# A recurrent cell with a chosen weight set: gate columns in groups of 256, 128 and 128, and the input-gate term written into PSUM by ScalarE

## The chip, the cores and the metric

One core of a Trainium2 chip runs the whole program. The metric is the device time of one execution in microseconds (us). The kernel before takes 7033.68 us, the median of 2 runs (7032.79 and 7034.57).

## The reference, cut to what matters

The program is a chain of eight layers over 625 nodes of 512 features. The change lies in one of them, a recurrent layer that walks over the 625 rows one after the other. At each row it first chooses one of four cells from the state, and then applies that cell alone:

```python
def step(carry, x_t):
    h, c = carry
    logits = concatenate([h, c, x_t]) @ W_sel.T + b_sel      # 4 logits
    s = argmax(logits)                                       # the chosen cell
    g = x_t @ W_ih[s] + h @ W_hh[s] + b_ih[s] + b_hh[s]      # 2048 values: i, f, g, o
    i, f, g, o = split(g, 4)
    c2 = sigmoid(f) * c + sigmoid(i) * tanh(g)
    h2 = sigmoid(o) * tanh(c2)
    return (h2, c2), h2
```

Nothing of a step can begin before the h and c of the step before it are there, and the cell is known only when the logits are.

## The kernel before, in words

`stage_lstm` (L1517 to L1845) holds the recurrence. TensorE, VectorE, ScalarE, GpSimd and SyncE each run a program of their own, which semaphores keep together; the order on each engine is that of the code, written out by hand. The loops hold `UN = 2` steps each: 312 turns of two steps after a first cell. The products with the input, `x_t @ W_ih` for all cells, lie ready in device memory (`xg`); SyncE loads the 64 values per partition of a coming step into `xg_buf`.

On TensorE a step goes as follows (`turn_of_two`, L1759 on).

- The logits: one matmul for the input's share (L1764), four with the new c as weights (L1767, after `c_ready`), four with tanh(c) as weights (L1772, after `w_ready` and `tanh_c`). They are 32-bit, so each is two passes, and leaves two weight loads and two matmuls in the trace.
- The products with h: h stands as two 16-bit parts in `h_pair`, four columns of weights, and W_hh streams past. A group of them (`products`, L1774) is four matmuls side by side on the four column quarters of the array, one for each quarter j of 512 gate columns. The 512 columns are cut in two: the first `FIRST = 320` go into `ps_rows`, the other 192 into `ps_rows_last`. A full sum is eight groups (two parts of W_hh, four chunks of h).
- The first `AHEAD = 2` chunks are multiplied for all four cells before the choice is known: 8 groups of 320 columns. Then TensorE waits for `best` (the index that VectorE finds, L1642), loads the index into a register and branches into one of four copies of `recurrent` (L1802): 6 more groups of 320 columns, 8 groups of 192 columns, and four 32-bit matmuls with a unit matrix that put the chosen cell's input term into `ps_gates` (L1806).
- The turns: the rows of gates (4 partitions wide) are copied to `gate_rows` by ScalarE (320 columns, L1701) and VectorE (192 columns, L1649), and 16 small 32-bit matmuls with `l_gsel` turn them into columns and add them to `ps_gates` (L1823): 10 after ScalarE's copy (`evac_a`), 6 after VectorE's (`evac_v`).
- The late products: two 32-bit matmuls of 156 columns (L1835) per step, a piece of `x @ W_ih` for rows that come much later.

The gate values are interleaved: each of the 16 columns of `ps_gates` holds one gate of one chunk, and a quarter of 512 columns mixes the gates. So ScalarE's tanh over all 16 columns (L1685) waits for all turns. Then come on VectorE the input and forget part (L1626), the output gate (L1627), the new c (L1629) and the gated selection weights (L1631); on ScalarE tanh(c) (L1687); on VectorE h twice and its second 16-bit part (L1634, L1635, L1637), which TensorE's next groups wait for (`hp_ready`). ScalarE follows the same branch as TensorE (L1695 to L1714), since which cell's rows it copies depends on the index.

Of the kernel before, what the change touches and what calls it, by code (L numbers as in the profile page):

```python
# [1426 lines left out]
GATE_SLOT = (0, 1, 3, 2)  # L1427
SLOT_GATE = (0, 1, 3, 2)
# [5 lines left out]
def stage_input_gates(nc, xt, wih_in, bias_a_in, bias_b_in, bias, scale, xg):  # L1434
# [4 lines left out]
    with ExitStack() as ctx:  # L1439
# [10 lines left out]
        with nc.Block() as block:  # L1450
# [32 lines left out]
            def _(v):  # L1483
                nc.vector.memset(scale[:], 0.5).then_inc(S["bias"], 1)
                v.wait_ge(S["bias"], 1)
                nc.vector.memset(scale[:].rearrange("p (s q) -> p s q", s=CELLS)[:, :, 3 * KC:], 1.0).then_inc(S["bias"], 1)
# [37 lines left out]
def stage_lstm(nc, whh, xt, wih_in, bias, scale, xg, xsel, pairs, wsel, ident, gsel, hist):  # L1524
# [9 lines left out]
    FIRST = 5 * 64  # L1534
    assert 1 + LOOPS * UN == N
    TURNS, PER, GROUP = BLOCK // UN, KC // UN, 2 * KC
    with ExitStack() as ctx:
        def sb(name, shape, dt=F32):
            return ctx.enter_context(nc.sbuf_tensor(name, shape, dt))
        xgb = sb("xg_buf", [128, UN, 2, CELLS * 8])  # L1540
# [4 lines left out]
        act = sb("gates_and_c", [128, 20])  # L1545
        ccur = act[:, 16:20]
# [9 lines left out]
        psg = ctx.enter_context(nc.psum_tensor("ps_rows", [128, CELLS * BANK], F32))  # L1556
        psb = ctx.enter_context(nc.psum_tensor("ps_rows_last", [128, BANK], F32))
        psc, psl = (ctx.enter_context(nc.psum_tensor(n, [128, BANK], F32)) for n in ("ps_gates", "ps_logits"))
# [4 lines left out]
            "xg0_in", "init", "c_ready", "o", "w_ready", "h_made", "hp_ready", "logits", "best", "rows_first", "rows_last", "evac_a", "evac_v",  # L1563
            "gates", "acted", "fi", "tanh_c", "kept", "seen_v", "seen_a", "seen_g", "seen_pe", "xg_used", "late_used", "late_moved", "late_stored")}
        with nc.Block() as block:
            @block.sync
            def _(sp):
                sp.dma_start(xg0[:].rearrange("p (h e) -> p h e", h=2), xg[0, :, :, 0, :].rearrange("h p e -> p h e")).then_inc(S["xg0_in"], 16)

                def load_gates(g, token):  # L1570

                    for h in range(2):
                        sp.dma_start(xgb[:, g, h, :].rearrange("p (s e) -> p s e", s=CELLS), xg[:, h, :, ds(token, 1), :].rearrange("s p t e -> p s (t e)")).then_inc(xg_in[g], 16)
# [40 lines left out]
            def _(v):  # L1614
                nc.vector.memset(hpair[:], 0.0).then_inc(S["init"], 1)
                for e in range(CELLS):
                    nc.vector.memset(psg[:, e * BANK:(e + 1) * BANK], 0.0).then_inc(S["init"], 1)
                nc.vector.memset(psb[:], 0.0).then_inc(S["init"], 1)
                nc.vector.memset(ccur, 0.0).then_inc(S["init"], 1)
                v.wait_ge(S["init"], CELLS + 3)  # L1620

                def cell(k):
# [8 lines left out]
                    nc.vector.tensor_tensor(wgated[:], wsel[:, 0:KC, :], ok[:].unsqueeze(2).broadcast_to([128, KC, PAIRS]), ALU.mult).then_inc(S["w_ready"], 1)  # L1631

# [49 lines left out]
            def _(a):  # L1682
                def cell(k):
                    a.wait_ge(S["gates"], k + 1)
                    nc.scalar.activation(act[:, 0:16], psc[:, 0:16], ACT.Tanh).then_inc(S["acted"], 1)  # L1685
# [4 lines left out]
                with a.Fori(0, LOOPS) as i:  # L1690
                    for q in range(UN):
# [58 lines left out]
            def _(pe):  # L1750
                pe.wait_ge(S["init"], CELLS + 3)
# [6 lines left out]
                nc.tensor.matmul(psc[:, 0:16], ident[:], xg0[:], start=True, stop=True).then_inc(S["gates"], 1)  # L1758
                def turn_of_two(i, token):  # L1759

                    for q in range(UN):
# [13 lines left out]
                        def products(e, part, c, out, lo, hi):  # L1775

                            for j in range(4):
                                at = e * CELL_COLS + (part * KC + c) * GATES + j * D
                                m = nc.tensor.matmul(out[32 * j:32 * j + 4, :], hpair[:, c, 2 - 2 * part:6 - 2 * part], whh[:, at + lo:at + hi],  # L1779
                                                     start=(part == 0 and c == 0), stop=(part == 1 and c == KC - 1), skip_group_check=True)  # L1780
                            return m

                        def first(e, part, c):

                            return products(e, part, c, psg[:, e * BANK:e * BANK + FIRST], 0, FIRST)

# [8 lines left out]
                        def recurrent(e):  # L1795
# [24 lines left out]
                        def turn(c, quarters=range(4)):  # L1820

                            for j in quarters:
                                m = nc.tensor.matmul(psc[32 * j:32 * j + 32, c:16:4], gsb[:, c * 128 + 32 * j:c * 128 + 32 * j + 32], gsel[:], start=False, stop=(c == KC - 1), skip_group_check=True)  # L1823
                            return m

# [511 lines left out]
```

## Time and profile before

| what | value |
|---|---|
| median of 2 runs | 7033.68 us |
| profiled execution, own time | 7026.58 us |
| its span in the trace | 7024.9 us |
| TensorE busy (matmul) | 6144.5 us, 87% of the span |
| VectorE, ScalarE, GpSimd busy | 2459.5, 1721.2, 928.1 us |
| mean granted TensorE clock | 0.961 of full |
| recurrent stage in the trace | about 3584 to 6660 us |

Busy time of TensorE includes the draining of its pipeline, so it is no measure of how close the engine is to its limit. In a step of a few microseconds, what matters is the order of the waits: which engine stands idle until which event. The profile's line number is that of the instruction's source line, so all products with h stand under L1779, told apart by the PSUM tile that they write.

### The profile page before, as it was taken

How to read it: one execution, taken by the hardware profiler on the slowest of the kernel's cores; microseconds unless marked ns; L12 is line 12 of the kernel's file. 1: busy time of each engine (PE TensorE's matmuls, PEld its weight loads, DVE VectorE, ACT ScalarE, POOL GpSimd, SP SyncE). 2: the span in 40 equal slices, each digit the busy share in tenths (PEclk: the TensorE clock that was granted, in tenths of full speed). 3: DMA queues.
4: the chain of work that ended last, by engine and by line, in shares of the span. 5: the costliest groups of instructions: out<-in, count | busy, mean ns of one | idle time of the engine just before them, and what ended most of it. 6: DMA issues, size and time to landing. Idle time of an engine off the chain costs nothing. (4 is left out here: it accounts for less than half of the span.)

```text
span 7024.9 us, 492334 instructions
## 1 busy us (share of the span) xinstructions
PE 6144.5 (87%) x210539; PEld 4079.7 (58%) x210539; DVE 2459.5 (35%) x11546; ACT 1721.2 (25%) x8472; POOL 928.1 (13%) x2082
## 2 busy tenths in 40 slices
PE   6856999999999999998789999999999999999852
PEld 5523555555555545544467777777777777777631
DVE  5324545455542211111233332333333332222248
ACT  0121333333333333333011111111111111111112
POOL 0011111111118820000000000000000000000003
PEclk9977999999999999999799999999999999999975
DMA  1011111111111100000232221222112221111100
GB/s 48 1 45 35 33 33 34 33 34 33 34 35 42 42 7 0 0 0 0 71 94 41 40 41 16 40 41 45 22 31 44 42 35 7 7 7 7 16 20 8
DMA packets 806866, 204.14 MB, mean 29 GB/s; under 512 B 701431, under 2 KB 766683, under 8 KB 806804
## 3 DMA queue, kind: packets, MB, share of 16 engines
q1 hardware_dynamic: 764500, 151.79, 11.3%
q0 software_dynamic: 41152, 46.42, 2.4%
q10 hardware_dynamic: 1152, 5.15, 0.2%
q8 instruction: 35, 0.57, 0.0%
q14 instruction: 27, 0.22, 0.0%
HBM read 174.86 MB, written 28.16 MB: 29 GB/s over the span
## 5 line engine op out<-in xcount | busy, mean ns | idle before, releaser
L1779 PE MATMUL ps_rows<-whh,h_pair 128*4 128x320 f16 x34944 | 1305.9, 299 | 84.2 <-issue 2.4
L1095 PE MATMUL ode_busy<-ode_busy_x,ode_busy_w 128*32 128x320 f16 (+4 forms) x19248 | 1244.8, 320 | 9.1 <-PEq L1031 7.1
L1779 PEld LDWEIGHTS ps_rows<-whh,h_pair 128*4 128x4 f16 x34944 | 735.2, 84 | 511.0 <-DVE h_pair L1637 154.2
L1089 PEld LDWEIGHTS ode_psa<-ode_a,ode_w2t 128*32 128x32 f32 x19968 | 396.6, 108 | 770.8 <-ACT ode_a L1204 573.2
L1649 DVE COPY gate_rows<-ps_rows_last 128x192 f32<-128x192 f32 x624 | 222.9, 357 | 1511.8 <-PE ps_rows_last L1779 1511.8
L1214 DVE SCALAR_TENSOR_TENSOR ode_part<-ode_b 128x1 f32<-128x1 f32 x624 | 111.5, 179 | 1645.1 <-ACT ode_b L1206 1643.3
L1701 ACT COPY gate_rows<-ps_rows 128x320 f32<-128x320 f32 x624 | 265.8, 426 | 1676.7 <-PE ps_rows L1779 1676.7
L1089 PE MATMUL ode_psa<-ode_a,ode_w2t 128*32 128x1 f32 x19968 | 607.0, 181 | 49.4 <-ACT ode_a L1198 43.2
L1206 ACT ACTIVATE ode_b<-ode_psa 128x1 f32<-128x1 f32 x2496 | 427.4, 171 | 815.9 <-PE ode_psa L1089 799.1
L1823 PE MATMUL ps_gates<-l_gsel,gate_rows 128*32 128x4 f32 x19968 | 397.4, 176 | 147.2 <-DVE gate_rows L1649 147.1
L1779 PE MATMUL ps_rows_last<-whh,h_pair 128*4 128x192 f16 x19968 | 521.4, 246 | 0.0
L1835 PE MATMUL ps_late<-l_xt,late_w 128*128 x2496 | 496.6, 321 | 0.0
L1106 PE MATMUL ode_pso<-whh 125*32 125x170 f32 (+1 forms) x8160 | 473.7, 310 | 0.0
L1204 ACT ACTIVATE ode_a<-ode_psu 128x1 f32<-128x1 f32 x1872 | 320.9, 171 | 595.9 <-PE ode_psu L1089 595.9
L1089 PE MATMUL ode_psa<-ode_ones,ode_b_parts 128*32 128x1 bf16 x9988 | 458.3, 163 | 0.0
L1779 PEld LDWEIGHTS ps_rows_last<-whh,h_pair 128*4 128x4 f16 x19968 | 429.2, 85 | 49.9
L1823 PEld LDWEIGHTS ps_gates<-l_gsel,gate_rows 128*32 128x32 f32 x19968 | 297.9, 110 | 202.3 <-DVE gate_rows L1649 202.0
L1724 POOL COPY l_hist<-h_now 128x4 f32 x624 | 117.2, 188 | 2094.8 <-DVE h_pair L1635 2086.8
L1095 PEld LDWEIGHTS ode_busy<-ode_busy_x,ode_busy_w 128*32 128x32 f16 x19248 | 378.8, 95 | 22.7 <-issue 10.1
L1835 PEld LDWEIGHTS ps_late<-l_xt,late_w 128*128 128x128 f32 x2496 | 351.2, 188 | 16.4
L1089 PE MATMUL ode_psu<-ode_b,ode_mt_half 128*32 128x1 f32 x9984 | 303.4, 181 | 30.0
L1089 PEld LDWEIGHTS ode_psu<-ode_b,ode_mt_half 128*32 128x32 f32 x9984 | 198.1, 108 | 192.1 <-ACT ode_b L1206 189.4
(505 smaller groups left out, 9500.7 us busy)
## 6 DMA issues: line engine op xcount, KB each, us to landing
late_w<-in_wih_t SPq DMA_DIRECT2D x386, 128.0 KB, 2.1
xg_buf<-xg_scratch SPq DMA_DIRECT2D x1248, 16.0 KB, 2.0
split_raw<-in_whh_t SPq DMA_DIRECT2D x64, 256.0 KB, 2.6
ig_w<-in_wih_t SPq DMA_DIRECT2D x8, 2048.0 KB, 11.5
xg_scratch<-late_out SPq DMA_DIRECT2D x24, 624.0 KB, 3.2
whh<-h_scratch SPq DMA_DIRECT2D x90, 62.5 KB, 2.3
xg_scratch<-ig_out ACTq DMA_DIRECT2D x8, 628.0 KB, 8.1
h_scratch<-mlp_h SPq DMA_DIRECT2D x40, 125.0 KB, 2.3
```

The costliest lines, as they stand in the source:

```text
L1089: m = nc.tensor.matmul(ps[32 * j:32 * j + 32, 0:1], w[:, 32 * j:32 * j + 32], col, start=start, stop=stop, skip_group_check=True)
L1095: nc.tensor.matmul(ps_busy[32 * j:32 * j + 32, 0:cols], busy_w[:, 32 * j:32 * j + 32], busy_x[:, 0:cols], start=True, stop=True, skip_grou ...
L1106: m = nc.tensor.matmul(acc[b][lo:hi, lo_col:hi_col], B["hot"][a][:, lo:hi], B["m"][a][:, b * BANK + lo_col:b * BANK + hi_col], start=(a == ...
L1204: nc.scalar.activation(a_col[:], ps_u[:, 0:1], ACT.Tanh).then_inc(S["a"], 1)
L1206: nc.scalar.activation(b_col[r][:, s:s + 1], ps_a[:, 0:1], ACT.Tanh).then_inc(S["b"], 1)
L1214: nc.vector.scalar_tensor_tensor(part[:], b[:, 1:2], 2.0, b[:, 0:1], ALU.mult, ALU.add).then_inc(S["s"], 1)
L1649: nc.vector.tensor_copy(gsb[:, FIRST:D], psb[:, 0:D - FIRST]).then_inc(S["evac_v"], 1)
L1701: nc.scalar.copy(gsb[:, 0:FIRST], psg[:, e * BANK:e * BANK + FIRST]).then_inc(S["evac_a"], 1)
L1724: nc.gpsimd.tensor_copy(hist[:, ds(k, 1), :], hcur[:]).then_inc(S["kept"], 1)
L1779: m = nc.tensor.matmul(out[32 * j:32 * j + 4, :], hpair[:, c, 2 - 2 * part:6 - 2 * part], whh[:, at + lo:at + hi], start=(part == 0 and c ...
L1823: m = nc.tensor.matmul(psc[32 * j:32 * j + 32, c:16:4], gsb[:, c * 128 + 32 * j:c * 128 + 32 * j + 32], gsel[:], start=False, stop=(c == K ...
L1835: m = nc.tensor.matmul(ps_late[:, 0:BLOCK], late_w[:, c * 128:(c + 1) * 128], xt[:, c, ds(token, BLOCK)], start=(c == 0), stop=(c == KC - 1))
```

## The change

The gate columns are regrouped by gate. W_hh's columns are laid out on the host as blocks i, g, f, o (`BLOCK_GATE`), and the 512 columns of a quarter are cut into 256 (input gate and candidate), 128 (forget gate) and 128 (output gate), with a PSUM bank each for the forget and the output part. VectorE copies the two 128-column parts one after the other. The turns go gate by gate: i and g after ScalarE's copy, f after `evac_f`, which releases a tanh over 12 columns, and o after `evac_o`, which releases a tanh of its own over 4 columns, in another bank. VectorE makes c from the first tanh, and the output gate and the gated selection weights from the second. The four unit-matrix matmuls of `recurrent` are gone: ScalarE copies the chosen cell's 16 input values into both gate banks right after its branch, and the turns add to that. `AHEAD` stays 2. Host layout, the selection weights' scale and the constants of `l_gsel` follow.

```diff
-    FIRST = 5 * 64
+    FIRST = 2 * 128
+    IFG = 3 * KC
...
-        psg = ctx.enter_context(nc.psum_tensor("ps_rows", [128, CELLS * BANK], F32))
-        psb = ctx.enter_context(nc.psum_tensor("ps_rows_last", [128, BANK], F32))
+        psg = ctx.enter_context(nc.psum_tensor("ps_rows", [128, CELLS * FIRST], F32))
+        psf, pso = (ctx.enter_context(nc.psum_tensor(n, [128, BANK], F32)) for n in ("ps_rows_forget", "ps_rows_out"))
+        pscq = ctx.enter_context(nc.psum_tensor("ps_gates", [128, 2, BANK], F32))
+        psc, psq = pscq[:, 0, 0:16], pscq[:, 1, 0:16]
...
             def _(v):
...
-                    nc.vector.scalar_tensor_tensor(parts[:], act[:, 0:8], 1.0, act[:, 12:20], ALU.add, ALU.mult).then_inc(S["fi"], 1)
-                    nc.vector.tensor_scalar(ok[:], act[:, 8:12], 1.0, 1024.0, ALU.add, ALU.mult).then_inc(S["o"], 1)
+                    nc.vector.scalar_tensor_tensor(parts[:], act[:, 0:2 * KC], 1.0, act[:, 2 * KC:4 * KC], ALU.add, ALU.mult).then_inc(S["fi"], 1)
                     v.wait_ge(S["fi"], k + 1)
                     nc.vector.scalar_tensor_tensor(ccur, parts[:, KC:2 * KC], 0.5, parts[:, 0:KC], ALU.mult, ALU.add).then_inc(S["c_ready"], 1)
+                    v.wait_ge(S["out_acted"], k + 1)
+                    nc.vector.tensor_scalar(ok[:], out_tanh[:], 1.0, 1024.0, ALU.add, ALU.mult).then_inc(S["o"], 1)
+                    nc.vector.scalar_tensor_tensor(wgated[:], out_tanh[:].unsqueeze(2).broadcast_to([128, KC, PAIRS]), 1.0, wsel[:, 0:KC, :], ALU.add, ALU.mult).then_inc(S["w_ready"], 1)
...
-                    v.wait_ge(S["rows_last"], k)
-                    nc.vector.tensor_copy(gsb[:, FIRST:D], psb[:, 0:D - FIRST]).then_inc(S["evac_v"], 1)
+                    v.wait_ge(S["rows_forget"], k)
+                    nc.vector.tensor_copy(gsb[:, 256:384], psf[:, 0:128]).then_inc(S["evac_f"], 1)
+                    v.wait_ge(S["rows_out"], k)
+                    nc.vector.tensor_copy(gsb[:, 384:512], pso[:, 0:128]).then_inc(S["evac_o"], 1)
...
             def _(a):
                 def cell(k):
                     a.wait_ge(S["gates"], k + 1)
-                    nc.scalar.activation(act[:, 0:16], psc[:, 0:16], ACT.Tanh).then_inc(S["acted"], 1)
+                    nc.scalar.activation(act[:, 0:IFG], psc[:, 0:IFG], ACT.Tanh).then_inc(S["acted"], 1)
+                    a.wait_ge(S["out_gate"], k + 1)
+                    nc.scalar.activation(out_tanh[:], psq[:, IFG:16], ACT.Tanh).then_inc(S["out_acted"], 1)
...
                         def move(e):
+                            nc.scalar.copy(pscq[:, :, 0:16], xgb[:, q, e * 16:(e + 1) * 16].unsqueeze(1).broadcast_to([128, 2, 16])).then_inc(S["xg_used"], 1)
                             a.wait_ge(S["rows_first"], k)
-                            nc.scalar.copy(gsb[:, 0:FIRST], psg[:, e * BANK:e * BANK + FIRST]).then_inc(S["evac_a"], 1)
+                            nc.scalar.copy(gsb[:, 0:FIRST], psg[:, e * FIRST:(e + 1) * FIRST]).then_inc(S["evac_a"], 1)
...
                         def recurrent(e):
...
                             for part in range(2):
                                 for c in range(KC):
-                                    m = products(e, part, c, psb[:, 0:D - FIRST], FIRST, D)
-                            m.then_inc(S["rows_last"], 1)
-                            for j in range(4):
-                                m = nc.tensor.matmul(psc[32 * j:32 * j + 32, 0:16], ident[:, 32 * j:32 * j + 32], xgb[:, q, :, e * 8:(e + 1) * 8], start=True, stop=False, skip_group_check=True)
-                            m.then_inc(S["xg_used"], 1)
+                                    m = products(e, part, c, psf[:, 0:128], 256, 384, (part, c) == (0, 0))
+                            m.then_inc(S["rows_forget"], 1)
+                            for part in range(2):
+                                for c in range(KC):
+                                    m = products(e, part, c, pso[:, 0:128], 384, 512, (part, c) == (0, 0))
+                            m.then_inc(S["rows_out"], 1)
...
                         pe.wait_ge(S["evac_a"], k)
-                        turn(0)
-                        turn(1)
-                        turn(2, (0, 1))
-                        pe.wait_ge(S["evac_v"], k)
-                        turn(2, (2, 3))
-                        turn(3).then_inc(S["gates"], 1)
-
-                        for c in range(q * PER, (q + 1) * PER):
-                            m = nc.tensor.matmul(ps_late[:, 0:BLOCK], late_w[:, c * 128:(c + 1) * 128], xt[:, c, ds(token, BLOCK)], start=(c == 0), stop=(c == KC - 1))
-                        m.then_inc(S["late_used"], 1)
+                        turn(psc[:, 0:KC], 0, False)
+                        turn(psc[:, 2 * KC:3 * KC], 1, False)
+                        pe.wait_ge(S["evac_f"], k)
+                        turn(psc[:, KC:2 * KC], 2, True).then_inc(S["gates"], 1)
+                        pe.wait_ge(S["evac_o"], k)
+                        turn(psq[:, IFG:16], 3, True).then_inc(S["out_gate"], 1)
+                        late(0)
+                        late(1)
```

`turn` now makes four 32-bit matmuls for one gate, and `late(n)` is one of the two late products, unchanged.

## Rows read from the trace of the kernel before

**Rows 1.** Windows: stretch, its us, busy PE, PEld, DVE, ACT, POOL, clock, DMA.

```profile
3604.00:6600.00 2996.00, 2771.32 (x91399) 2137.13 (x91390) 963.28 (x5675) 496.76 (x1828) 229.18 (x1219) 1.00 0.19 29
```

**Rows 2.** Timeline, 5000 to 5013 us: start, us, engine, line, count, [idle before].

```profile
5003.22 2.07 PE L1779 MATMUL ps_rows<-whh,h_pair 128*4 128x320 f16 x56
...
5005.12 0.83 PE L1779 MATMUL ps_rows_last<-whh,h_pair 128*4 128x192 f16 x32
5005.35 0.43 ACT L1701 COPY gate_rows<-ps_rows 128x320 f32<-128x320 f32 x1 [2.66 <-PE ps_rows L1779]
...
5005.78 0.22 PE L1806 MATMUL ps_gates<-xg_buf,ident 128*32 128x16 f32 x8
5005.82 0.27 PEld L1823 LDWEIGHTS ps_gates<-l_gsel,gate_rows 128*32 128x32 f32 x20
...
5006.01 0.36 DVE L1649 COPY gate_rows<-ps_rows_last 128x192 f32<-128x192 f32 x1 [2.71 <-PE ps_rows_last L1779]
5006.42 0.21 PEld L1823 LDWEIGHTS ps_gates<-l_gsel,gate_rows 128*32 128x32 f32 x12 [0.33 <-DVE gate_rows L1649]
...
5006.65 0.80 PE L1835 MATMUL ps_late<-l_xt,late_w 128*128 x4
5006.77 0.18 ACT L1685 ACTIVATE gates_and_c<-ps_gates 128x16 f32<-128x16 f32 x1 [0.99 <-PE ps_gates L1823]
...
5007.18 0.16 DVE L1629 SCALAR_TENSOR_TENSOR gates_and_c<-input_and_forget_part 128x4 f32<-128x4 f32 x1
...
5007.37 0.09 PEld L1764 LDWEIGHTS ps_logits<-l_pairs,xsel_now 128*1 128x1 f32 x2 [0.16 <-issue]
...
5007.64 0.35 PE L1772 MATMUL ps_logits<-wsel_out_gate,tanh_c 128*1 128x16 f32 x8
...
5007.90 0.17 DVE L1637 TENSOR_TENSOR h_pair<-h_now,h_pair 128x4 f16<-128x4 f32 x1
...
5008.03 0.16 DVE L1642 TENSOR_REDUCE best_hits<-ps_logits 1x4 uint8<-1x16 f32 x1
5008.12 0.91 PEld L1779 LDWEIGHTS ps_rows<-whh,h_pair 128*4 128x4 f16 x32 [0.25 <-DVE h_pair L1637]
5008.12 2.10 PE L1779 MATMUL ps_rows<-whh,h_pair 128*4 128x320 f16 x56
5009.23 0.65 PEld L1779 LDWEIGHTS ps_rows<-whh,h_pair 128*4 128x4 f16 x24 [0.19 <-issue]
```

**Rows 3.** Line L1779, idle time of its engine before it: us, times.

```profile
  issue: 70.2, 335
```

**Rows 4.** Groups by line, 3604 to 6600 us: count, busy us, mean ns.

```profile
L1649 DVE COPY gate_rows<-ps_rows_last 128x192 f32<-128x192 f32 x610 | 217.9, 357 | 1468.8 <-PE ps_rows_last L1779 1468.8
L1631 DVE TENSOR_TENSOR wsel_out_gate<-l_wsel,out_gate 128x64 f32<-128x64 f32 x609 | 136.1, 223 | 0.0
```

**Rows 5.** Timeline of weight loads in the loop's first turn, 3583 to 3601 us.

```profile
3589.18 1.16 PEld L1779 LDWEIGHTS ps_rows<-whh,h_pair 128*4 128x4 f16 x24 [2.54 <-issue]
...
3595.80 0.65 PEld L1779 LDWEIGHTS ps_rows<-whh,h_pair 128*4 128x4 f16 x24 [0.56 <-issue]
...
3599.12 0.14 PEld L1806 LDWEIGHTS ps_gates<-xg_buf,ident 128*32 128x32 f32 x3 [1.72 <-issue]
```

**Rows 6.** DMA queues in that turn, 3584 to 3604 us: packets, MB.

```profile
q8 instruction: 5, 0.08, 1.7%
```

**Rows 7.** DMA queues from then on, 3604 to 6600 us, all of them.

```profile
q1 hardware_dynamic: 701581, 85.47, 18.8%
q14 instruction: 2, 0.02, 0.0%
```

**Rows 8.** DMA queues in the loop of an earlier layer (L1246), 660 to 2095 us, all.

```profile
q0 software_dynamic: 37184, 42.69, 10.7%
q1 hardware_dynamic: 6720, 5.38, 1.6%
```

More of the change, by code:

```diff
@@ L1539, in sb @@
             return ctx.enter_context(nc.sbuf_tensor(name, shape, dt))
-        xgb = sb("xg_buf", [128, UN, 2, CELLS * 8])
+        xgb = sb("xg_buf", [128, UN, CELLS * 16])
         xg0 = sb("xg_first", [128, 16])
@@ L1562, in stage_lstm @@
         S = {k: new_semaphore(nc, "lstm_" + k) for k in (
[L1563 to L1564 removed]
+            "xg0_in", "init", "c_ready", "o", "w_ready", "h_made", "hp_ready", "logits", "best", "rows_first", "rows_forget", "rows_out", "evac_a", "evac_f", "evac_o",
+            "gates", "out_gate", "acted", "out_acted", "fi", "tanh_c", "kept", "seen_v", "seen_a", "seen_g", "seen_pe", "xg_used", "late_used", "late_moved", "late_stored")}
         with nc.Block() as block:
@@ L1756, in _ @@
                 pe.wait_ge(S["kept"], 1)
-                nc.tensor.matmul(psc[:, 0:16], ident[:], xg0[:], start=True, stop=True).then_inc(S["gates"], 1)
+                nc.tensor.matmul(psc, ident[:], xg0[:], start=True, stop=True).then_inc(S["gates"], 1)
+                nc.tensor.matmul(psq, ident[:], xg0[:], start=True, stop=True).then_inc(S["out_gate"], 1)
                 def turn_of_two(i, token):
@@ L1773, in turn_of_two, with products @@
                         m.then_inc(S["logits"], 1)
-                        def products(e, part, c, out, lo, hi):
+                        def products(e, part, c, out, lo, hi, start):
                             for j in range(4):
@@ L1779, in products @@
                                 m = nc.tensor.matmul(out[32 * j:32 * j + 4, :], hpair[:, c, 2 - 2 * part:6 - 2 * part], whh[:, at + lo:at + hi],
-                                                     start=(part == 0 and c == 0), stop=(part == 1 and c == KC - 1), skip_group_check=True)
+                                                     start=start, stop=(part == 1 and c == KC - 1), skip_group_check=True)
                             return m
                         def first(e, part, c):
-                            return products(e, part, c, psg[:, e * BANK:e * BANK + FIRST], 0, FIRST)
+                            return products(e, part, c, psg[:, e * FIRST:(e + 1) * FIRST], 0, FIRST, part == 0 and c == 0 and e % 2 == 0)
                         pe.wait_ge(S["hp_ready"], k)
@@ L1818, in turn_of_two, with turn, late @@
                                 recurrent(0)
-                        def turn(c, quarters=range(4)):
-                            for j in quarters:
-                                m = nc.tensor.matmul(psc[32 * j:32 * j + 32, c:16:4], gsb[:, c * 128 + 32 * j:c * 128 + 32 * j + 32], gsel[:], start=False, stop=(c == KC - 1), skip_group_check=True)
-                            return m
-                        pe.wait_ge(S["evac_a"], k)
-                        turn(0)
-                        turn(1)
-                        turn(2, (0, 1))
-                        pe.wait_ge(S["evac_v"], k)
-                        turn(2, (2, 3))
-                        turn(3).then_inc(S["gates"], 1)
-                        for c in range(q * PER, (q + 1) * PER):
-                            m = nc.tensor.matmul(ps_late[:, 0:BLOCK], late_w[:, c * 128:(c + 1) * 128], xt[:, c, ds(token, BLOCK)], start=(c == 0), stop=(c == KC - 1))
-                        m.then_inc(S["late_used"], 1)
+                        def turn(out, block_no, last):
+                            for j in range(4):
+                                m = nc.tensor.matmul(out[32 * j:32 * j + 32, :], gsb[:, block_no * 128 + 32 * j:block_no * 128 + 32 * j + 32], gsel[:, int(block_no == 1), :],
+                                                     start=False, stop=last, skip_group_check=True)
+                            return m
+                        def late(n):
+                            c = q * PER + n
+                            m = nc.tensor.matmul(ps_late[:, 0:BLOCK], late_w[:, c * 128:(c + 1) * 128], xt[:, c, ds(token, BLOCK)], start=(c == 0), stop=(c == KC - 1))
+                            if n == PER - 1:
+                                m.then_inc(S["late_used"], 1)
+                        pe.wait_ge(S["evac_a"], k)
+                        turn(psc[:, 0:KC], 0, False)
[6 more added lines that the diff above has]
+                        late(1)
                 assert LOOPS == (BLOCKS + 1) * TURNS
@@ L2316, in lay_out @@
     a["pairs"] = pairs.reshape(128, PAIRS)
-    gsel = np.zeros((128, 4), np.float32)
-    for j in range(4):
-        half = 1.0 if j == 2 else 0.5
-        gsel[32 * j:32 * j + 2, GATE_SLOT[j]] = half * 2.0 ** -17
-        gsel[32 * j + 2:32 * j + 4, GATE_SLOT[j]] = half * 2.0 ** -28
+    gsel = np.zeros((128, 2, KC), np.float32)
+    for j in range(KC):
+        for b, half in enumerate((0.5, 1.0)):
+            gsel[32 * j:32 * j + 2, b, j] = half * 2.0 ** -17
+            gsel[32 * j + 2:32 * j + 4, b, j] = half * 2.0 ** -28
     a["gsel"] = gsel
```

39 lines of the change are left out of this document (20 added, 19 removed).

## The prediction, made before the result was known

> **What bounds the kernel now.** The windows come first. In the recurrent stage the clock stands at 1.00, so TensorE runs at 2.4 GHz there, and 2996 us hold 610 steps [rows 1, 4]: 4.91 us a step, 624 steps after the first cell. A change of 0.1 us in a step is worth 62 us, 0.9% of the run. Nothing else of the program is touched beyond its setup.
>
> Then one step in the timeline [rows 2]. Two rings of waits close in it, and both take about 4.9 us.
>
> The h ring. TensorE starts the products at 5003.22 and streams until 5005.78; VectorE's copy starts at 5006.01, the last turns at 5006.42, the tanh at 5006.77, the last piece of h ends at 5008.07 and the next products start at 5008.12. Period: 4.90.
>
> The choice ring. Behind its last turns TensorE runs the late products (5006.65), and the logits queue behind them: their first weight load at 5007.37 comes 0.03 after c is done (5007.18 + 0.16), which looks like a wait for c, but it is not the matmul that waits for c, and its idle time is put down to issue. Four late matmuls and a pause of 0.16 fill the stretch from 5006.65. The logits end at 5007.99, the index at 5008.19, and TensorE's first weight load behind the branch comes at 5009.23, that is 1.04 after the index. What hides the branch is the work ahead: 8 groups from 5008.12.
>
> That the two rings are nearly equal shows in line L1779: its weight loads stood idle 335 times "until issue", 0.21 us each [rows 3]. In about half of the steps the branch comes a little late, in the others the work ahead just covers it. So shortening the h ring alone gains nothing; the choice ring must get shorter too.
>
> **The change part by part.** Durations are of one execution of 7026.58 us, with a span of 7024.9; it is 7.1 below the median of 7033.68.
>
> *Products.* In the step without a pause, 14 groups of 320 columns take 5005.12 - 5003.22 = 1.90, 135.7 ns each, and 8 of 192 columns 5005.78 - 5005.12 = 0.66, 82.5 ns each [rows 2]. The difference is 0.416 ns a column, which is 2.4 GHz, with 2.7 ns over. Estimates from that: 109.1 ns for 256 columns, 55.9 for 128. Behind the branch: before 6 x 135.7 + 8 x 82.5 = 1.474; after 6 x 109.1 + 16 x 55.9 = 1.549. That is +0.075 in the choice ring, as 24 groups now bear the fixed part in place of 14. Ahead of the branch: 8 x 26.6 = 0.21 less.
>
> Bounds for the 128-column group: 55.9 if it streams; 82.5, as the 192-column group, if each group has to wait for its weight loads. I take 55.9, because pairs with almost nothing to stream are much faster: twenty pairs of the turns go within 0.27 [rows 2], less some 0.11 for one load, so 8.4 ns a pair, 34 ns for four.
>
> The Trainium skill ("TensorE: Matmul & The Clock Gate", Back-to-back issue gap) speaks against the change here: it puts a stream of weight load and matmul pairs at about 81 ns for 128 columns, against some 56 for matmuls alone. By the first figure a step would hold 0.40 more; the row of 192 columns, 82.5 ns of which 80 are streaming, shows no such floor on top of the stream, but can't exclude one under it.
>
> *Copies.* VectorE's copy of 192 columns takes 357 ns, an operation on 64 takes 223 [rows 4]: 1.05 ns a column, so 290 for 128. The one on the path is that of the output part: -0.067. Bounds 223 and 357. The forget part's copy lies beside the output part's products (8 x 55.9 = 0.45). ScalarE's copy shrinks from 0.43, and starts 0.16 earlier; two further product parts follow, so it is covered.
>
> *Turns.* Behind VectorE's last copy there are 4 matmuls, 8 pairs, where 6 with 12 were: 4 x 8.4 ns, -0.034. The others run beside that copy.
>
> *Input term.* Four unit-matrix matmuls leave TensorE; they ran before the copy came (5005.78 against 5006.42), so that gains nothing. On ScalarE a copy of 2 x 16 values comes in, between 0.18 (L1685, 16 columns) and 0.43 (L1701, 320). ScalarE stands idle for 2.66 before its rows copy [rows 2], so 0. It also releases `xg_buf` earlier, so SyncE's two loads go out earlier; nothing else is queued behind them on that engine but loads.
>
> *Gates.* Before, the tanh starts 0.99 after the products' end (5005.78 to 5006.77). After, 24 pairs of turns (0.20), the drain of the last one (5006.42 + 0.29 less 12 pairs, some 0.18) and 0.05 to ScalarE make 0.43, as no copy stands between: an estimate of -0.56 for the h ring, on top of the products. ScalarE's wait for the output turns stands ahead of tanh(c), and VectorE's wait for the second tanh ahead of the output gate, the selection weights and h. That tanh starts some 0.45 after the first one, by the copy in between: about when c is done, so tanh(c) and h slip by 0.1 at most. The h ring, of 4.90, loses 0.56 and the 0.14 that 14 x 109.1 + 16 x 55.9 is shorter than 2.56, and gets to 4.2; with what the work ahead no longer covers of the branch (0.87 against some 1.06) to 4.4.
>
> *The choice ring.* The late products stand behind the output turns, and the logits behind these, as before. So this ring sees only +0.075 - 0.067 - 0.034 = -0.026 up to the index. From index to products it is 1.04 where a pause shows, and no more than 1.02 in the other step (5003.29 to 5003.22 + 8 x 0.1357 = 5004.31). I take 0.99 against a mean of 1.03, as the 8 groups ahead are handed out well before the index now and no longer hold up the read of it: -0.04. Bounds: 0.90, if handing them out cost more than it seems, and 1.04.
>
> *Sum.* The ring that ends last is the choice ring: -0.066 a step, 624 steps: -41 us; 7026.58 - 41 = 6985, and with the 7.1 to the median about 6992. Forecast: 6990. In a sentence: the change takes some 0.5 us off the ring through h, and the ring through the choice gives nearly all of it back as a pause before the branch. Setup (two of six fills less, one scaling less) is 0. Its own range: with the bounds of branch and copy, 6900 to 7060.
>
> **Rivals.**
>
> *A. The loop's code is fetched again (slower).* In the loop's first turn the weight loads stop three times "until issue", for 2.54, 0.56 and 1.72 us [rows 5], while five packets of instructions come in, 0.08 MB [rows 6]; from then on TensorE's queue q8 moves nothing [rows 7]. So the loop of some 1,395 instructions (counted in the code: 342 pairs a step, and a few) stays near the engine. The change makes each of the four copies 88 pairs in place of 64, and the loop some 1,779. For: all of it grows by 28%, and no row shows a loop of that size being kept. Against: an earlier loop of some 1,520 runs 1435 us without one such packet [rows 8], so the limit isn't near the old size. It decides at the size where the end of the loop drives out its start. Price: from one stop of 1.72 per turn to all three, 4.82: 312 x 1.72 = 537 to 1504 us, 7530 to 8490. The Trainium skill ("Runtime: NRT & Kernel Launch", Instruction fetch mechanics) gives TensorE room for 2048 instructions in blocks of 256, fetched ahead in sequence; by it 1,779 fit, but in eight blocks of eight, with none left for the one that is fetched ahead. The trace agrees on the block, five of 16 KB in 0.08 MB; no run here shows the room.
>
> *B. Weight loads set the pace of 128-column groups (slower).* 16 x (82.5 - 55.9) = +0.43 behind the branch, net +0.36: +225 us on 7033.68, 7260. Against it speaks the 8.4 ns a pair.
>
> *C. The choice ring does not bind (faster).* If the logits come no later than c allows, the step is the h ring plus the branch's rest, near 4.45 with some slip: 624 x 0.46 = 287, 6750. It would need TensorE to run the logits ahead of the late products, and nothing in the rows shows matmuls passing one another.
>
> **How the numbers follow.** Forecast 0.73, A 0.16, B 0.06, C 0.05. The range 6890 to 7260 holds the forecast with its bounds and B; A and C are left out, two in ten. Two per cent is about what a measurement of this kernel can tell from no change: below 6893 is faster, above 7174 slower. Faster 0.05 (C), slower 0.22 (A and B), same 0.73.
>
> **What would show it.** Right: 128-column groups at 56 ns; a pause of 0.4 to 0.5 us "until issue" before the weight loads behind the branch in every step, where 0.21 in half of them stood; TensorE's first products starting where the logits end, and no longer 0.05 after h; steps of 4.85. A shows as packets on q8 all through the stage; B as groups of 82 ns; C as steps under 4.6 with the logits ahead of the late products. The forecast is wrong if the branch costs other than 0.9 to 1.04 from the index, or if the longer idle time brings the clock of the stage below 1.00.

## The result, and the profile after

The changed kernel takes **12791.64 us** (2 runs, 12786.92 to 12796.35) against 7033.68: ratio 1.819, 95% interval [1.816, 1.822]. The prediction said 6990, and 6890 to 7260: wrong by far. Rival A, the loop's code fetched again, came true, at almost four times the highest price it had been given: 12,792 - 7,034 = 5,758 us, over 312 turns 18.5 us a turn. Its mark stands in the profile's page. PEclk has 40 slices of the span (tenths of the full clock); the queue's row gives packets, MB and share of time:

```profile
PEclk9799999999865556555555555555555555555556
...
q8 instruction: 2808, 46.01, 1.7%
```

The recurrent stage begins in slice 12. The queues of 3600 to 12400 us, which answer to [rows 7]:

```profile
q1 hardware_dynamic: 714391, 86.00, 6.7%
q8 instruction: 2769, 45.37, 2.4%
q14 instruction: 2, 0.02, 0.0%
```

In that stretch the loop makes 8800 / 28.3 = 311 turns: **8.9 packets of 16 KB a turn**, 2,280 instructions for a loop of 1,779, where before there were none. The windows (columns as in [rows 1]) of the first 3 ms:

```profile
3604.00:6600.00 2996.00, 1522.48 (x37236) 1158.90 (x37236) 420.58 (x2233) 228.99 (x1070) 80.02 (x428) 0.58 0.10 18
```

The clock is 0.58 of full, a mean of its two levels and close to the lower one, 1.2 GHz; before it was 1.00 [rows 1]. In this stretch TensorE stood still some six times a turn, mostly for 1.3 to 3.7 us, as the rows below show. What the weight loads waited for, 3700 to 12300 us (us in total, times, longest):

```profile
PEld ps_rows L1791 <- issue: 2060.5, 630, 7.3
PEld ps_logits L1776 <- issue: 1146.3, 607, 4.8
PEld ps_gates L1836 <- issue: 952.0, 501, 4.0
PEld ps_rows_forget L1791 <- issue: 394.8, 265, 2.5
PEld ps_logits L1784 <- issue: 313.1, 291, 2.0
PEld ps_rows_out L1791 <- issue: 46.3, 36, 2.7
```

No engine, semaphore or transfer of data is named: "issue" is a wait for nothing that the profile shows. In all 4,913 us over 8600 / 28.3 = 304 turns, 16.2 a turn. One turn in the timeline:

```profile
6003.12 0.96 PEld L1791 LDWEIGHTS ps_rows<-whh,h_pair 128*4 128x4 f16 x24 [3.70 <-issue]
...
6009.35 0.08 PEld L1784 LDWEIGHTS ps_logits<-wsel_out_gate,tanh_c 128*1 128x1 f32 x1 [1.30 <-issue]
...
6014.04 0.96 PEld L1791 LDWEIGHTS ps_rows<-whh,h_pair 128*4 128x4 f16 x24 [3.67 <-issue]
...
6017.49 0.30 PEld L1791 LDWEIGHTS ps_rows_forget<-whh,h_pair 128*4 128x4 f16 x13 [1.74 <-issue]
...
6021.50 0.53 PEld L1836 LDWEIGHTS ps_gates<-l_gsel,gate_rows 128*32 128x32 f32 x32 [2.86 <-issue]
...
6026.64 0.11 PEld L1776 LDWEIGHTS ps_logits<-l_pairs,xsel_now 128*1 128x1 f32 x2 [3.58 <-issue]
```

There are two kinds of place: behind a branch (3.70 and 3.67 into the chosen copy, 2.86 out of it, 3.58 back to the top), and in straight code, within one run of equal instructions (1.30 and 1.74). The two straight ones lie behind instruction 7,618 and 8,130, counted in the program, 512 apart: two of the seams between blocks of 256. Counted from these seams the loop begins 101 instructions behind a seam and ends 87 instructions into its eighth block; these places, here and below, are good to one or two instructions.

### The profile page after: what moved, and what is told of

Its sections match the earlier page's. It is cut to its first block and busy times, and to the rows that moved or that the text cites. A ratio compares the mean times of both kernels' runs of the same rounds, so it can differ in the third digit from the quotient of the medians.

```text
span 12785.0 us, 524786 instructions
## 1 busy us (share of the span) xinstructions
PE 7801.6 (61%) x225517; PEld 5303.7 (41%) x225517; DVE 2653.9 (21%) x12168; ACT 1879.0 (15%) x9721; POOL 925.8 (7%) x2082
## 5 line engine op out<-in xcount | busy, mean ns | idle before, releaser
L1791 PE MATMUL ps_rows<-whh,h_pair 128*4 128x256 f16 x34944 | 1949.1, 387 | 1835.2 <-issue 1835.2
L1791 PEld LDWEIGHTS ps_rows<-whh,h_pair 128*4 128x4 f16 x34944 | 1144.3, 108 | 2333.7 <-issue 2118.0
L1655 DVE COPY gate_rows<-ps_rows_forget 128x128 f32<-128x128 f32 x624 | 182.1, 292 | 4276.7 <-PE ps_rows_forget L1791 4276.7
L1791 PE MATMUL ps_rows_forget<-whh,h_pair 128*4 128x128 f16 x19968 | 732.3, 306 | 326.2 <-issue 326.2
L1843 PE MATMUL ps_late<-l_xt,late_w 128*128 x2496 | 773.9, 456 | 0.0
L1791 PEld LDWEIGHTS ps_rows_forget<-whh,h_pair 128*4 128x4 f16 x19968 | 562.5, 121 | 488.5 <-issue 403.1
L1791 PE MATMUL ps_rows_out<-whh,h_pair 128*4 128x128 f16 x19968 | 688.0, 307 | 37.8 <-issue 37.3
L1712 ACT COPY gate_rows<-ps_rows 128x256 f32<-128x256 f32 x624 | 232.5, 373 | 3004.0 <-PE ps_rows L1791 3004.0
L1791 PEld LDWEIGHTS ps_rows_out<-whh,h_pair 128*4 128x4 f16 x19968 | 568.2, 126 | 47.3 <-issue 47.3
L1843 PEld LDWEIGHTS ps_late<-l_xt,late_w 128*128 128x128 f32 x2496 | 562.9, 289 | 11.0
```

The source lines that it names most:

```text
L1655: nc.vector.tensor_copy(gsb[:, 256:384], psf[:, 0:128]).then_inc(S["evac_f"], 1)
L1712: nc.scalar.copy(gsb[:, 0:FIRST], psg[:, e * FIRST:(e + 1) * FIRST]).then_inc(S["evac_a"], 1)
L1843: m = nc.tensor.matmul(ps_late[:, 0:BLOCK], late_w[:, c * 128:(c + 1) * 128], xt[:, c, ds(token, BLOCK)], start=(c == 0), stop=(c == KC - 1))
```

## The experiments

Theories: **F**, the code is fetched anew because of how many blocks the loop touches; **R**, the new order of gates, banks and tanhs costs it; **N**, a limit on the number of instructions alone. Ratios are to the kernel before, run beside them, with 95% intervals.

**1 and 2. The kernel before, only longer.** Harmless matmuls in the seldom chosen copies, 24 or 28 each:

```diff
                             m.then_inc(S["rows_first"], 1)
+                            if e != 1:
+                                for _ in range(24):      # 28 in the second
+                                    nc.tensor.matmul(psb[0:4, D - FIRST:D - FIRST + 1], hpair[:, 0, 2:6], whh[:, 0:1], start=False, stop=False, skip_group_check=True)
```

> Theory F (the loop's code is fetched anew in every turn): instructions come in blocks of 256 at fixed places, since the stops of the changed kernel that follow each other in the code lie 512 instructions apart (after instruction 7,618 and 8,130, counted without labels), and a loop is kept as long as its blocks and the one behind them are at most eight. This is the kernel before, with 24 tiny matmuls more in each of the copies for cells 0, 2 and 3, which are chosen in 89 of 624 steps: 1,683 instructions a turn, ending at 8,372, in seven blocks; with the one behind them eight. F expects 7035 to 7060 us (89 steps by at most 0.3 us), clock 1.00 and no instruction packets in the stage. Theory R (the new order of gates, banks and tanhs is what costs) expects the same here. Theory N (a limit on the number of instructions alone, anywhere between 1,520 and 1,779) expects about 12,800 if the limit is below 1,683.

> As the run with 24, with 28 tiny matmuls in each of the three copies: 48 instructions more, 1,731 a turn, ending at 8,420, in eight blocks, with the one behind them nine. F expects 312 turns by some 16 to 20 us of stops more: 12,000 to 13,300 us, q8 with eight to nine packets a turn, the clock of the stage near 0.5. R expects 7035 to 7065, since nothing of the change is in it. N expects 12,800 only if its limit lies in or below these 48 instructions.

Measured: 7094.34, ratio 1.008 [1.006, 1.010], and **10191.57**, 1.449 [1.446, 1.452]. Queues of both from 3620 to 6500 us, 24 first:

```profile
q1 hardware_dynamic: 666359, 84.37, 18.9%
q14 instruction: 2, 0.02, 0.0%
```

```profile
q1 hardware_dynamic: 340338, 52.92, 10.8%
q8 instruction: 660, 10.81, 1.7%
q14 instruction: 1, 0.01, 0.0%
```

48 instructions more in copies that are seldom chosen cost 3.1 ms. R falls: nothing of the change is in this kernel. Both sizes were missed. The 58 us of the first are the padding's own run: steps with cell 1 stay at 4.91, the 88 others take 5.53 (0.62 x 88 = 55). The second fetches 4.5 packets a turn, half of what was expected.

**3. The changed kernel, moved by 160 instructions.**

```diff
+                for _ in range(40):
+                    nc.tensor.matmul(psl[:, 0:16], ident[:], xg0[:], start=True, stop=True, skip_group_check=True)
                 def turn_of_two(i, token):
```

> The changed kernel, with 40 matmuls (160 instructions) that nothing reads put ahead of the loop on TensorE, once. The loop has the same 1,779 instructions, but begins 5 instructions behind the start of a block instead of 101, and so touches seven blocks in place of eight. F expects the stops gone: no packets of q8 in the stage, clock 1.00, and the time that was forecast for the change, 6900 to 7060, most likely 6990 (plus about 5 for the 40 matmuls). R and N expect 12,790, as the loop and its order are unchanged.

Measured: **6966.18 us**, ratio 0.991 [0.989, 0.992]: the same loop, 5,825 us faster, and 0.9% faster than the kernel before. Its windows, its queues in the same stretch, and its waits:

```profile
3604.00:6590.00 2986.00, 2687.61 (x108348) 2238.73 (x108340) 1220.72 (x6415) 697.06 (x3112) 232.40 (x1244) 1.00 0.19 29
```

```profile
q1 hardware_dynamic: 714528, 86.12, 19.1%
q8 instruction: 5, 0.08, 0.0%
q14 instruction: 3, 0.02, 0.0%
```

```profile
PEld ps_rows L1793 <- issue: 350.8, 625, 3.2
PEld ps_gates L1838 <- DVE gate_rows L1657: 179.8, 622, 0.3
PEld ps_logits L1778 <- issue: 103.6, 622, 0.4
```

The five packets came in with the first turns: from 3620 us on there are none. With these, N falls as well: 1,779 instructions stay if they lie in seven blocks.

**4. Less code.** Each turn of 128 values as one matmul instead of four:

```diff
-                            for j in range(4):
-                                m = nc.tensor.matmul(out[32 * j:32 * j + 32, :], gsb[:, block_no * 128 + 32 * j:block_no * 128 + 32 * j + 32], gsel[...], ...)
+                            return nc.tensor.matmul(out, gsb[:, block_no * 128:(block_no + 1) * 128], gsel[...], ...)
```

> The changed kernel, with each turn of 128 gate values as one matmul of 128 columns of weights in place of four of 32: 96 instructions less a turn, 1,683, ending at 8,376, seven blocks. F expects no packets of q8 in the stage, clock 1.00, 6900 to 7100: against the aligned kernel a turn's pairs cost between 8 pairs of 8.4 ns (as before) and two loads of 55 ns and two drains, so up to 0.1 us a step (62 us) either way. R expects 12,790. N expects 6900 to 7100 if its limit lies between 1,683 and 1,779.

Measured: 7112.45, 1.011 [1.009, 1.013]; no packets behind the first turn. So less code cures it as well as another place does. The 0.25 us a step over the aligned kernel, put at 0.1 at most, was mis-sized: the weight loads of its turns run in its timeline as

```profile
5005.59 0.97 PEld L1835 LDWEIGHTS ps_gates<-l_gsel,gate_rows 128*128 128x128 f32 x8
```

They start 0.11 apart. In the aligned kernel the four loads of 32 columns that do the same work start 0.007 apart, and the next four 0.028 behind the first; the prediction's 8.4 ns a pair makes that 0.034.

**5, 11 and 12. Where exactly.** The aligned kernel with 43, 10 and 55 matmuls ahead of the loop in place of 40; some 3, 127 and 51 instructions lie in the eighth block.

> The aligned kernel with 43 in place of 40 matmuls ahead of the loop, so 12 instructions later: the loop of 1,779 begins 17 instructions behind the start of a block and its last two instructions, the branch back among them, lie in an eighth block. Theory F expects the stops back: nine blocks for room of eight, at least the 10.1 us a turn that the kernel with 1,731 instructions cost, up to the 18.7 of the changed kernel: 10,100 to 12,800 us, packets on q8 all through the stage. If instead the size or the place of most of the loop is what counts, or the aligned kernel is fast for another reason that the 40 matmuls bring (a PSUM bank written, a later start), this one takes 6960 to 6975 as well.

> The changed kernel with 10 matmuls ahead of the loop in place of the aligned kernel's 40: the same code, but the loop begins 141 instructions behind the start of a block and 127 of its instructions lie in an eighth block. Theory F as the runs left it (eight blocks can stay; what drives the first one out is the fetch of the ninth, behind the loop's end, and it goes out the more surely the longer TensorE is in the eighth block): at least as bad as the changed kernel with its 87, 12,700 to 13,400 us, some nine packets a turn on q8. Rival: the 40 matmuls themselves cure it (a bank written, a later start): then 10 of them bring 6965 to 9000.

> The changed kernel with 55 matmuls ahead of the loop: it begins 65 instructions behind the start of a block and 51 of its instructions lie in the eighth block, between the kernel with 1,731 instructions (35 there, 10.1 us a turn more) and the changed kernel (87, 18.7 us a turn). Theory F as above: 10,100 to 12,800 us, 4.5 to 9 packets a turn. Rival: more matmuls ahead of the loop cure it the better: 6970.

Measured: 7116.91 (7082.38 to 7151.44), **12728.91** and 7146.72 (7111.81 to 7181.64). The expectations of 5 and 12 failed, that of 11 held. q8 on the three pages:

```profile
q8 instruction: 118, 1.93, 0.1%
```

```profile
q8 instruction: 2827, 46.32, 1.6%
```

```profile
q8 instruction: 100, 1.64, 0.1%
```

Run 11 answers the rival that the added matmuls themselves cure it. Runs 5 and 12 show that a loop in eight blocks *can* stay for most turns: about 37 packets are the program's one pass (37 in run 3), which leaves 81 and 63. In run 5 the long turns come in nine places, in run 12 in seven, each a pair of some 14 and 24 us: **nine packets a time**. The 1,413 of run 2 make 157 times nine, as many as half the turns; the 2,770 of the changed kernel 308 times nine, nearly every turn. This reads as one event everywhere: one block from behind the loop comes in, and then all eight of the loop come in again, each taking the place of the next that is needed. The count of nine is measured; which blocks they are, no view shows. The price agrees too: (7149.8 - 6962.2 of the aligned kernel) / 9 = 20.8 us and (7110.2 - 6962.2) / 7 = 21.1 by the spans, (10191.57 - 7094.34) / 157 = 19.7, and in the changed kernel (12785.0 - 6962.2) / 312 = 18.7. The Trainium skill ("Runtime: NRT & Kernel Launch", Instruction fetch mechanics) describes TensorE's store as first in, first out, for 2048 instructions in blocks of 256; nine packets for one block too many is what such a store would show. That crossing a block's end is mostly hidden, as the same section has it, does not hold here, by the 1.30 and 1.74 us in straight code.

What lets the ninth block in stays open. In run 12 the seven turns are just those that choose cell 0, the last copy, in their second step; in run 5 two are the turns at which the inner loop of 78 begins anew, and seven choose cell 2 in their second step, though not all that do. In the two kernels in which it happens in nearly every turn the usual path (cell 1) jumps into the eighth block; in runs 2, 5 and 12 it runs into it. That was seen in one execution each, not tested. The path alone can't be all of it: the two executions of run 12 choose the same cells and lie 70 us apart, those of run 5 69, an estimated three events each.

**6 and 7. Which ring.** The second late product of a step, moved behind the next step's logits, in the aligned kernel and in the kernel before (counts of `late_used` follow):

```diff
                         m.then_inc(S["logits"], 1)
+                        late((2 * q - 1) % KC, token).then_inc(S["late_used"], 1)
...
-                        late(0)
-                        late(1)
+                        late(2 * q, token)
```

> The aligned kernel with the second late product of a step moved behind the next step's logits, ahead of its products with h; same instruction count and same place in the blocks. Two-ring theory: with the code kept, the choice ring sets the step (4.78 us, with a pause of 0.56 us before the branch), and the late products stand in it, 0.56 us of weight loads. Half of them leave: the logits can start 0.28 earlier, at the earliest 0.32 earlier, when the gated selection weights are there. In the new place the product costs at most the 0.13 us that it ends after h, which the pause covers. Expected: 0.20 to 0.30 us a step less, 6780 to 6840 us. Rival: the logits wait for c and not for the late products, so nothing moves or the products with h start 0.2 later: 6960 to 7100.

> The same move of the second late product in the kernel before. Two-ring theory: there the ring through h (4.90 us) does not contain the late products, and the steps take 4.90 to 4.93; so a shorter choice ring gains at most 0.03 us a step, and a product that ends up to 0.1 after h is there takes as much: 7010 to 7100 us. If the choice ring alone set the step before as well, the time falls by 0.2 to 0.3 us a step as in the aligned kernel: 6850 to 6910.

Measured: 7024.99, 1.000 [0.999, 1.001], and 7182.73, 1.022 [1.020, 1.023]: both misses, both slower than expected. Run 6:

```profile
5004.02 0.18 DVE L1643 TENSOR_TENSOR h_pair<-h_now,h_pair 128x4 f16<-128x4 f32 x1
5004.17 0.30 PEld L1774 LDWEIGHTS ps_late<-l_xt,late_w 128*128 128x128 f32 x2
5004.28 0.16 DVE L1648 TENSOR_REDUCE best_hits<-ps_logits 1x4 uint8<-1x16 f32 x1
...
5004.64 0.75 PEld L1799 LDWEIGHTS ps_rows<-whh,h_pair 128*4 128x4 f16 x32 [0.17 <-issue]
...
5005.66 0.54 PEld L1799 LDWEIGHTS ps_rows<-whh,h_pair 128*4 128x4 f16 x24 [0.28 <-issue]
```

h is there at 5004.20, and the products begin at 5004.64: a late product costs 0.30 and a pause of 0.17 behind it, which the expectation had left out. The pause before the branch, 0.28 here, is still there, so the choice ring still sets the step. By medians over all steps, the stretch from the output turns to the index is 0.19 shorter than in the aligned kernel (1.52 for 1.71), but from the index to the branch's first weight load it is 1.22 in place of 0.94. TensorE reads the index behind the products that it has ahead of the branch, and the read comes 0.48 after the index in place of 0.20. In run 7 the same stretch grows from 1.00 to 1.25, which is the whole loss of 0.25 a step. Nothing is gained there: from the last turns to the index it is 1.77 whether one late product stands there or two. The prediction's choice ring had the late products set the time of the logits; in the kernel before they do not. The last logits wait for tanh(c) there:

```profile
5007.38 0.20 ACT L1687 ACTIVATE tanh_c<-gates_and_c 128x4 f32<-128x4 f32 x1 [0.43 <-DVE gates_and_c L1629]
```

It ends at 5007.58, and their weight loads start at 5007.64 [rows 2]; by medians this is 0.05 in the kernel before and in run 7, and 0.44 in the aligned kernel, where the late products do set the time.

**8. The input term alone, in the kernel before.** ScalarE's copy in, the four unit-matrix matmuls out.

```diff
+                            nc.scalar.copy(psc[:, 0:16].rearrange("p (h e) -> p h e", h=2), xgb[:, q, :, e * 8:(e + 1) * 8]).then_inc(S["xg_used"], 1)
                             a.wait_ge(S["rows_first"], k)
...
-                            for j in range(4):
-                                m = nc.tensor.matmul(psc[32 * j:32 * j + 32, 0:16], ident[:, 32 * j:32 * j + 32], xgb[...], start=True, ...)
```

> The kernel before with one part of the change alone: ScalarE copies the chosen cell's 16 input values into PSUM, and the four unit-matrix matmuls leave TensorE (128 instructions less a turn, 1,267). The prediction put this part at 0: the matmuls ran before VectorE's copy was done, and ScalarE stands idle for 2.66 us before its rows copy. Expected 7020 to 7045. Rival: ScalarE's write comes late or holds up its copy of the rows: 0.2 us a step more, 7160; or the matmuls did delay the turns: up to 0.1 a step less, 6970.

Measured: 7028.19, 1.000 [0.999, 1.001]. As expected.

**9. Three chunks ahead**, in the aligned kernel: `AHEAD = 3`.

> The aligned kernel with three chunks of h in place of two multiplied for all four cells ahead of the choice: four groups of 256 columns more ahead of the branch, one less behind it; the instruction count stays. Two-ring theory: the aligned kernel's choice ring sets the step with a pause of 0.56 us before the branch, in which the four groups (4 x 0.109 = 0.44) are hidden, and the ring loses one group: 0.109 x 624 = 68 us, 6895 to 6905. If the groups in the queue hold up the read of the index, the branch comes later by as much as they are late, and the gain falls to nothing: 6966. If the ring through h set the step, the time would rise by 0.33 a step: 7170.

Measured: 7053.01, 1.003 [1.002, 1.004], slower than the aligned kernel by 87 us.

```profile
5002.60 1.19 PEld L1793 LDWEIGHTS ps_rows<-whh,h_pair 128*4 128x4 f16 x48
...
5002.80 0.16 DVE L1648 TENSOR_REDUCE best_hits<-ps_logits 1x4 uint8<-1x16 f32 x1 [0.25 <-PE ps_logits L1786]
...
5004.14 0.43 PEld L1793 LDWEIGHTS ps_rows<-whh,h_pair 128*4 128x4 f16 x20 [0.35 <-issue]
```

The index is there at 5002.96, the branch's first load comes 1.18 later, 0.95 in the aligned kernel. And yet TensorE pauses 0.35: the branch did not wait for the array but came late itself. The longer row of work ahead delays the read of the index by 0.23, the group saved gives back 0.11: +0.12 a step, 75 us. The trace has the read itself 0.43 after the index in place of 0.20. The mechanism was the second case of the expectation; but that case stopped at no gain, and this is a loss.

**10. One late product in the gap** ahead of the wait for VectorE's last copy, in the aligned kernel.

```diff
+                        late(0)
                         pe.wait_ge(S["evac_o"], k)
                         turn(psq[:, IFG:16], 3, True).then_inc(S["out_gate"], 1)
-                        late(0)
                         late(1)
```

> The aligned kernel with the first late product of a step put between the turns of the forget gate and the wait for VectorE's copy of the output part, where TensorE stands idle 0.29 us. From the run with the product behind the logits a late product costs 0.30 of weight loads and a pause of 0.17 behind it, 0.47 where nothing covers it. Here it ends 0.18 past the idle time, so the output turns, the second tanh and h come 0.18 later, while the logits lose 0.30 to 0.47 ahead of them. The choice ring gains 0.12 to 0.29 a step, as long as h is there in time: 6785 to 6890 us. Rival: the gated selection weights, which wait for the second tanh, become the last thing before the logits (0.32 from being so now): 0.02 to 0.14 a step is left, 6880 to 6955.

Measured: 6962.43, 0.990 [0.988, 0.992], no different from the aligned kernel. By medians the output turns come 0.19 later behind the index, and from them to the next index it is 0.20 less: the one takes what the other gives. The gated weights now end just before their logits (0.12, where it was 0.32), which is the rival's mechanism, with less left than it said:

```profile
5000.50 0.22 DVE L1635 SCALAR_TENSOR_TENSOR wsel_out_gate<-out_gate_tanh,l_wsel 128x64 f32<-128x64 f32 x1
...
5000.83 0.26 PEld L1786 LDWEIGHTS ps_logits<-wsel_out_gate,tanh_c 128*1 128x1 f32 x8
...
5002.49 0.54 PEld L1793 LDWEIGHTS ps_rows<-whh,h_pair 128*4 128x4 f16 x24 [0.49 <-issue]
```

The pause before the branch stays, 0.49 here and 0.36 in the median. Runs 3 and 10 beat the kernel before, by 0.9 and 1.0%.

## Why the prediction was wrong, point by point

**The step that failed** is rival A's dismissal, and with it the premise of the sum that the loop's code stays near the engine. "The limit isn't near the old size" was read from a loop of some 1,520 instructions. Size is not what decides: 1,779 stay in seven blocks (run 3), 1,731 do not in eight (run 2). The number that mattered had been in the text: "in eight blocks of eight, with none left for the one that is fetched ahead". But where the seams lie was not counted; by the places of the stops, the shortest cover of 1,779 is seven blocks and the old start gives eight.

**A's price** was mis-sized: 1.72 to 4.82 a turn, from the three stops of the first turn [rows 5], against 18.5. There the code came in once, with five packets [rows 6]; here nine come in nearly every turn, and the branches that stop in the turn above do so for 2.9 to 3.7. The wait on "issue" is 16.2 a turn, of which 454 us over 311 turns, 1.5, are in the aligned kernel too: 14.7 are stops. The remaining 4 of the 18.7 are put down to the lower clock by difference alone; what it does to the matmuls of the forget and output parts shows in the changed kernel:

```profile
6004.36 1.07 PE L1791 MATMUL ps_rows_forget<-whh,h_pair 128*4 128x128 f16 x32
6005.21 1.07 PE L1791 MATMUL ps_rows_out<-whh,h_pair 128*4 128x128 f16 x32
```

6005.21 - 6004.36 is 0.85 for eight groups, 106 ns each, where the aligned kernel takes 56 (below). "If the longer idle time brings the clock of the stage below 1.00" had named the clock, without a price, and for the pause before the branch.

**The forecast's own steps** are tested by run 3, where the code stays:

```profile
5003.93 0.17 DVE L1643 TENSOR_TENSOR h_pair<-h_now,h_pair 128x4 f16<-128x4 f32 x1
...
5004.15 0.76 PEld L1793 LDWEIGHTS ps_rows<-whh,h_pair 128*4 128x4 f16 x32
...
5004.36 0.16 DVE L1648 TENSOR_REDUCE best_hits<-ps_logits 1x4 uint8<-1x16 f32 x1 [0.26 <-PE ps_logits L1786]
...
5005.26 0.19 ACT L1710 COPY ps_gates<-xg_buf 128x32 f32<-128x32 f32 x1 [1.75 <-DVE best_hits L1648]
5005.47 0.54 PEld L1793 LDWEIGHTS ps_rows<-whh,h_pair 128*4 128x4 f16 x24 [0.56 <-issue]
5005.48 0.83 PE L1793 MATMUL ps_rows<-whh,h_pair 128*4 128x256 f16 x24 [0.28 <-issue]
...
5006.13 0.62 PE L1793 MATMUL ps_rows_forget<-whh,h_pair 128*4 128x128 f16 x32
...
5006.58 0.62 PE L1793 MATMUL ps_rows_out<-whh,h_pair 128*4 128x128 f16 x32
...
5007.25 0.29 DVE L1657 COPY gate_rows<-ps_rows_out 128x128 f32<-128x128 f32 x1 [0.15 <-PE ps_rows_out L1793]
...
5007.60 0.16 PEld L1838 LDWEIGHTS ps_gates<-l_gsel,gate_rows 128*32 128x32 f32 x8 [0.29 <-DVE gate_rows L1657]
...
5009.14 0.16 DVE L1648 TENSOR_REDUCE best_hits<-ps_logits 1x4 uint8<-1x16 f32 x1 [0.26 <-PE ps_logits L1786]
```

- *Products*: right. (5006.13 - 5005.48) / 6 = 108 ns for 256 columns, 0.45 / 8 = 56 for 128. So rival B is out, and the 81 ns that the Trainium skill ("TensorE: Matmul & The Clock Gate", Back-to-back issue gap) gives for 128 columns does not show.
- *Copies* 0.29, *input term* 0 (run 8 too): right. *Turns* were put at -0.034; from the start of the last turns to the late products it is 0.17 in place of 0.23.
- *Branch*: 0.99 expected from the index; 5005.47 - 5004.52 = 0.95, with a pause of 0.56 (350.8 / 625) in every step, 0.4 to 0.5 expected. The read of the index comes 0.20 behind it by medians, 0.25 before, as the prediction argued.
- *Sum*: from index to index 4.78; the means of all steps are 4.803, and 4.928 before: -0.125 for the -0.066 of the sum; the rest is the branch and the turns, some 0.03 each. 624 x 0.125 = 78 us. The 40 matmuls ahead of the loop, which the expectation of run 3 had put at about 5, take 17 back: from the first cell's unit-matrix matmul (L1770) to the first index it is 18.3, in the changed kernel 1.7. That leaves 61, where the spans differ by 7024.9 - 6962.2 = 63.
- *Which ring binds*: right for the changed order; the kernel before was misread on the late products (run 7). The pause before the branch stands in every step, and without it the ring through h would be 4.22 by medians (3.42 from the branch to h, 0.05 to the products, 0.75 for those ahead), against the 4.2 of the prediction. Runs 6, 9 and 10 each took work out of the choice ring and gained nothing, since the read of the index or the output turns came later by as much or more. C did not occur. One sign failed: the products still start 0.05 after h (5004.15 against 5003.93 + 0.17), as h and the logits end almost together.

## What to carry to other kernels

Before a loop on TensorE is made longer, count its instructions, all copies of a branch included, and the 16 KB blocks that they touch from where the loop starts: seven stayed in every run here, eight did so in most turns, in half or in hardly any. Packets on the instruction queue all through a stage, and stops "until issue" at fixed places of the code, are the mark of it; instructions put ahead of the loop can move it back, at the price of their own time. And a change should then be judged with its code in place: this one is worth 0.9%, and its first measurement said +82%.

## What the runs showed of the hardware that was not expected

- A loop on TensorE that touched one block of 256 instructions too many cost nine packets and 19 to 21 us at a time, as if all its blocks followed one another out.
- A stage at a clock of 1.00 ran at 0.58 once TensorE was stopped six times a turn, mostly for 1.3 to 3.7 us, and at 0.72 in run 2, with half the packets.
- Twelve groups in place of eight ahead of a branch delayed the read of its index by 0.23 us (run 9), and a start of the groups 0.37 later behind h delayed it by 0.28 (run 6), though TensorE stood idle before the branch for 0.35 and 0.28.
- 32-bit weight loads of 128 columns, with 4 columns to stream behind each, start 0.11 us apart (run 4); four of 32 columns with their matmuls take 0.028 (run 3).
